# Loads in the order of use, indirect stores behind the stacks' loads, and experts' rows one tile ahead: a change to a two-layer transformer kernel

## The chip, the cores and the metric

One NeuronCore of a Trainium2 chip. The metric is the device time of one execution in microseconds (us), as the median of several runs. PE is the matrix engine (PEld its weight loads), DVE the vector engine, ACT the scalar engine, POOL the GpSimd engine, and SP the engine that issues most of the DMAs. Each engine works through its own list of instructions in order; an instruction that waits holds up all that stand behind it.

## The reference

Sixteen sequences of 512 rows of 256 go through two layers. Every step is `x = x + f(layernorm(x))` but the last, which has no norm.

```python
q, k, v = split(norm(x) @ Wqkv)               # layer 0: 16 heads of 16, rotary positions
w = softmax(q k^T / 4, keys at most 127 back)
x = x + (w v) @ Wout
s = norm(x) @ Wr.T + br                       # 8 experts, each row goes to its top 2
x = x + sum over the 2 of weight_e * ((silu(a_e) * b_e) @ Wl2[e] + bl2[e])
q = norm(x) @ Wq.T + bq                       # layer 1: causal over all 512 keys, biases
k = norm(x) @ Wv.T + bv ; v = norm(x) @ Wk.T + bk
x = x + softmax(q k^T / 16) v @ Wo.T + bo
x = x + x @ (round(weight / s) clipped to -1..1, times s)
```

## The kernel before

The program has three stages, one after the other: **a0** (attention with a window, the routing, and the storing of the normed rows in `xs`, sorted by expert), the **experts** (39 tiles of 512 rows of `xs`, results to `ys`), and **a1** (the gathering of each row's two results from `ys`, full attention, the ternary product). a0 and a1 are the same function `pipeline`.

`pipeline` first runs a block of preparation (L335 to L414): SP loads w, the tables, the identity, the masks, `wo` in 16 pieces, and the rest; ACT and DVE split w into a high and a low part (`wh`, `wl`), DVE sets the rows of ones in both `kst`, and in a1 forms the bias `boa` and the ternary weights. All engines meet at its end. Only then comes the block that does the work, and with it the load of x (L488).

The work on a sequence is some 25 kinds of steps, and a written table, `turn(i)`, gives each step a position between 0 and 1 in a turn. In turn i four sequences are in work: i+2 is normed, turned over, projected, rotated (`rope`), split into three bf16 parts (`part`, POOL L579 to L590) and stored (SP L496) to `parts_dram`, from where it comes back in another layout as `qst` and `kst` (`stack`, SP L506, 8 loads of 384 KB); i+1 has its scores formed for the row maxima (`S`, PE L1073, DVE L882), which go through `nmax_dram` into `qst` (`minus`: SP L511, a wait for the store, SP L513); i has its exponentials and products (`T`, PE L1095, ACT L675, PE L1113); i-1 is turned back (PE L1127, ACT L691), multiplied by `wo` (PE L1136), and in a0 normed again, scored and routed. The steps of a turn are sorted by position, and every engine walks this one `order`.

In a0 the last step of a turn is `scatter` (position 0.97): POOL L563 issues 8 indirect DMAs of 128 rows each. The loads of the stacks stand at 0.70 to 1.0. SP also carries the experts' weights through the core: a load (`fetch`, L470), a split on ACT and POOL, a store (`keep`, L475).

In a1 `gather(n, k)` is 4 indirect DMAs in a row on POOL (L570) into the 4 tiles of one buffer `yg`, and `mix(n, k, t)` is DVE's product of a tile with its gate, added to x (L729). The first `mix` waits for all 4 gathers, and the next `gather` for all 4 `mix`. x is loaded at 0.55 of a turn, the gathers stand at 0.35 and 0.81, the statistics at the start of the next turn.

The experts' loop is two steps unrolled. In each SP issues for tile m the rows (`xg`, L1239), w1 (L1245), w2 (L1248) and two biases (L1251, L1252). On PE come the transposes of `xg` (L1396), the first product (L1360) and the second one (L1374) of an earlier tile. There is one `xg`.

Of the kernel before, what the change touches and what calls it, by code (L numbers as in the profile page):

```python
# [105 lines left out]
def pipeline(nc, name, x_in, x_out, w_all, w_out, tables, biases, window, scale, consts, routed, mixed, ternary_w):  # L106
# [19 lines left out]
    nmax_d = nc.dram_tensor(f"{name}_nmax_dram", [2, 2, H, T], BF16, kind="Internal").ap()  # L126
# [21 lines left out]
    def turn(i):  # L148
# [11 lines left out]
        if 0 <= o < B:  # L160
# [3 lines left out]
            out += [(0.16 + 0.02 * t, ("stats2", o, t)) for t in range(NT)] + [(0.235, ("aggr2", o))]  # L164
            if routed:
                out += [(0.28 + 0.02 * t, ("norm2", o, t)) for t in range(NT)]
                out += [(0.15, ("y", o)), (0.50, ("turn2", o, 0)), (0.52, ("turn2", o, 1)), (0.58, ("score", o)),
                        (0.66, ("exp2", o)), (0.79, ("place", o)), (0.97, ("scatter", o))]
                out += [(0.615 + 0.0175 * k, ("gates", o, k)) for k in range(20)]
            else:  # L170
                out += [(0.27 + 0.015 * t, ("norm2", o, t)) for t in range(NT)]
                out += [(0.345, ("turn2", o, 0)), (0.36, ("turn2", o, 1)), (0.49, ("last", o, 0)), (0.51, ("last", o, 1)),
                        (0.515, ("final", o, 0)), (0.535, ("final", o, 1)), (0.54, ("y", o))]
# [11 lines left out]
        for n, at in ((m, -0.5),) * (m == 0) + ((m + 1, 0.55),) * (0 <= m + 1 < B):  # L185
            out.append((at, ("load", n)))
            if mixed:
                out += [(at - 0.2, ("gather", n, 0)), (at + 0.26, ("gather", n, 1))]
                out += [(at + 0.19 + 0.02 * t, ("mix", n, 0, t)) for t in range(NT)]
                out += [(at + 0.39 + 0.015 * t, ("mix", n, 1, t)) for t in range(NT)]  # L190
            else:
                out += [(at + 0.25 + 0.02 * t, ("stats", n, t)) for t in range(NT)] + [(at + 0.33, ("aggr", n))]
        if biases and 0 <= m < B:
            out.append((0.50, ("shift", m)))
        if 0 <= m < B:
            if mixed:
                out += [(0.005 + 0.02 * t, ("stats", m, t)) for t in range(NT)] + [(0.075, ("aggr", m))]
                out += [(0.125 + 0.015 * t, ("norm", m, t)) for t in range(NT)]
            else:
                out += [(0.03 + 0.02 * t, ("norm", m, t)) for t in range(NT)]  # L200
            out += [(0.20, ("turn", m, 0)), (0.215, ("turn", m, 1))]
            for a in range(2):
                p = 0.27 + 0.13 * a
# [6 lines left out]
    for i in range(-2, B + 1):  # L210
# [6 lines left out]
    with ctx:  # L217
# [34 lines left out]
        bvc = xn[:, 0, :].rearrange("p (c n) -> p c n", c=KC)  # L252
        bob = xn[:, 1, :]
        all_ones = xn[:, 2, 0:P]
# [21 lines left out]
        ot = sb("ot", [P, KC, T])  # L276
        if routed:
# [1245 lines left out]
```

## Time and profile before

| | us |
|---|---|
| median of 3 runs | 3257.35 (3247.95 to 3259.71) |
| the profiled execution | 3238.48 |
| its span | 3236.8 |
| busy PE, DVE, ACT, POOL | 2606.6, 1855.1, 1375.3, 922.1 |
| mean granted clock of PE | 0.90 |
| a0, from start to the last scatter's first DMA | 0 to 1101 |
| experts, first transposes to the start of a1 | 1130 to 1916 |
| a1 | 1916 to 3237 |

A row of the timeline has the start, the duration, engine, line and operation, out<-in, the count of instructions put together, and in brackets the idle time before it with what ended it; "issue" is a wait for nothing that the profile shows.

### The profile page before, as it was taken

How to read it: one execution, taken by the hardware profiler on the slowest of the kernel's cores; microseconds unless marked ns; L12 is line 12 of the kernel's file. 1: busy time of each engine (PE TensorE's matmuls, PEld its weight loads, DVE VectorE, ACT ScalarE, POOL GpSimd, SP SyncE). 2: the span in 40 equal slices, each digit the busy share in tenths (PEclk: the TensorE clock that was granted, in tenths of full speed). 3: DMA queues.
4: the chain of work that ended last, by engine and by line, in shares of the span. 5: the costliest groups of instructions: out<-in, count | busy, mean ns of one | idle time of the engine just before them, and what ended most of it. 6: DMA issues, size and time to landing. Idle time of an engine off the chain costs nothing. (4 is left out here: it accounts for less than half of the span.)

```text
span 3236.8 us, 51965 instructions
## 1 busy us (share of the span) xinstructions
PE 2606.6 (81%) x17726; PEld 1745.3 (54%) x17726; DVE 1855.1 (57%) x6538; ACT 1375.3 (42%) x2419; POOL 922.1 (28%) x862
## 2 busy tenths in 40 slices
PE   3788888888888399989899952788888888888887
PEld 2455555555555277778777851344444444444444
DVE  3767766775675344444444443666666666666661
ACT  1445544554554233333333311255555545555554
POOL 2434544544342200000000004343333333334300
PEclk8889988988899699999999975799999989999998
DMA  4565565565433565566666544334444433333330
GB/s 118 164 199 169 190 202 166 166 210 194 145 126 99 186 239 212 214 217 215 214 214 214 215 137 117 102 102 123 131 120 128 122 106 106 106 105 111 100 93 14
DMA packets 263344, 494.65 MB, mean 153 GB/s; under 512 B 27104, under 2 KB 194272, under 8 KB 253024
## 3 DMA queue, kind: packets, MB, share of 16 engines
q1 hardware_dynamic: 245232, 437.99, 42.3%
q0 software_dynamic: 17904, 54.02, 5.0%
q8 instruction: 114, 1.87, 0.2%
q14 instruction: 94, 0.77, 0.1%
HBM read 302.53 MB, written 189.40 MB: 152 GB/s over the span
## 5 line engine op out<-in xcount | busy, mean ns | idle before, releaser
L882 DVE CUSTOM_DVE_ANT_0 a_junk<-a_bank,a_smask 128x256 bf16<-128x256 f32 (+3 forms) x2048 | 812.8, 435 | 499.5 <-PE a_bank L1073 477.2
L675 ACT ACTIVATE a_pr<-a_bank 128x512 f32<-128x512 f32 (+1 forms) x1152 | 635.7, 574 | 698.6 <-PE a_bank L994 636.3
L1073 PE MATMUL a_bank<-a_kst,a_qst 96*128 96x256 bf16 (+3 forms) x2048 | 464.8, 302 | 203.1 <-DVE a_nmax L882 149.6
L1095 PE MATMUL a_bank<-a_qst,a_kst 98*128 98x256 bf16 (+3 forms) x2048 | 440.4, 292 | 24.9 <-ACT a_pr L675 21.5
L1073 PEld LDWEIGHTS a_bank<-a_kst,a_qst 96*128 96x128 bf16 x2048 | 172.3, 102 | 457.9 <-DVE a_nmax L882 263.0
L1360 PE MATMUL e_bank<-e_xh,e_w 128*128 128x512 f32 x1248 | 402.9, 405 | 1.4 <-DVE e_xl L1341 1.4
L1113 PE MATMUL a_bank<-a_pr,a_va 128*32 128x256 f32 (+3 forms) x4096 | 365.9, 435 | 40.9 <-ACT a_pr L675 36.5
L994 PE MATMUL a_bank<-a_mask,a_identb 128*128 128x512 bf16 (+2 forms) x1152 | 356.1, 309 | 0.0
L1333 DVE SCALAR_TENSOR_TENSOR e_gf<-e_bank,e_b,e_sa 128x512 f32<-128x512 f32 x156 | 117.2, 751 | 280.5 <-ACT e_sa L1304 280.5
L1095 PEld LDWEIGHTS a_bank<-a_qst,a_kst 98*128 98x128 bf16 x2048 | 183.1, 101 | 152.5 <-ACT a_pr L675 72.0
L1304 ACT ACTIVATE e_sa<-e_bank,e_b 128x512 f32<-128x512 f32 x156 | 107.4, 689 | 371.5 <-PE e_bank L1360 371.3
L1360 PEld LDWEIGHTS e_bank<-e_xh,e_w 128*128 128x128 f32 x1248 | 237.3, 195 | 50.5 <-DVE e_xl L1341 1.8
L1360 PE MATMUL e_bank<-e_xl,e_w 128*128 128x512 f32 x624 | 250.3, 401 | 0.0
L1282 POOL DMA_DIRECT2D ys<-e_yt x39 | 29.5, 757 | 771.2 <-DVE e_yt L1322 752.1
L1374 PE MATMUL e_bank<-e_w,e_gh 128*128 128x256 f32 x1248 | 222.8, 279 | 2.9 <-DVE e_gl L1337 2.9
L1374 PEld LDWEIGHTS e_bank<-e_w,e_gh 128*128 128x128 f32 x1248 | 193.0, 189 | 4.9 <-DVE e_gl L1337 3.4
L1113 PEld LDWEIGHTS a_bank<-a_pr,a_va 128*32 128x32 f32 x4096 | 84.8, 111 | 186.9 <-issue 92.6
L570 POOL DMA_INDIRECT a_yg<-ys,a_yrow x128 | 124.2, 970 | 196.8 <-DVE a_xt L729 137.5
L1374 PE MATMUL e_bank<-e_w,e_gl 128*128 128x256 f32 x624 | 173.8, 279 | 0.0
L1337 DVE TENSOR_TENSOR e_gl<-e_gf,e_gh 128x512 fp32r<-128x512 f32 x156 | 108.1, 693 | 109.9 <-ACT e_gh L1309 109.9
L882 DVE DVE_READ_ACCUMULATOR2_ANT a_nmax<- 128x1 f32 x2048 | 169.7, 83 | 0.0
L1136 PE MATMUL a_bank<-a_wo,a_ot 128*128 128x256 f32 x512 | 155.2, 457 | 15.5 <-ACT a_ot L691 14.7
(168 smaller groups left out, 4494.7 us busy)
## 6 DMA issues: line engine op xcount, KB each, us to landing
e_w<-ws_dram SPq DMA_DIRECT2D x39, 2048.0 KB, 9.5
a_parts_dram<-a_parts SPq DMA_DIRECT2D x224, 256.0 KB, 4.0
a_qst<-a_parts_dram SPq DMA_DIRECT2D x128, 384.0 KB, 9.9
a_kst<-a_parts_dram SPq DMA_DIRECT2D x128, 384.0 KB, 11.1
e_w<-ws_dram SPq DMA_DIRECT2D x39, 1024.0 KB, 6.0
a_parts_dram<-a_parts SPq DMA_DIRECT2D x32, 768.0 KB, 3.8
ws_dram<-a_ws SPq DMA_DIRECT2D x24, 1024.0 KB
e_xg<-xs SPq DMA_DIRECT2D x39, 512.0 KB, 6.0
```

Source lines behind the costliest of these rows:

```text
L570: pool.indirect_dma_start(yg[:, t, :], None, ys, bass.IndirectOffsetOnAxis(ap=yrow[:, k, m * NT + t:m * NT + t + 1], axis=0))\
L675: nc.scalar.activation(pr[b][:, h:h + per, :], TB_[at % 2][:, 0:per * w].rearrange("p (h w) -> p h w", h=per), ACT.Exp, scale=scale).then_ ...
L882: last = nc.vector.tensor_tensor_reduce(junk[:, at % 2, j * w:(j + 1) * w], SB_[at % 2][:, j * w:(j + 1) * w], smask[:, T - w:T], scale=-1 ...
L994: return nc.tensor.matmul(out, identb[:, :], rhs, start=False, stop=True, skip_group_check=True)
L1073: last = nc.tensor.matmul(out[:, j * w:(j + 1) * w], q[0:ROWS, hh, qb * P:(qb + 1) * P], k[0:ROWS, hh, k0:k0 + w], start=True, stop=True)
L1095: nc.tensor.matmul(out[:, j * w:(j + 1) * w], k[0:AUG, hh, b * P:(b + 1) * P], q[0:AUG, hh, q0:q0 + w], start=(j == 0), stop=False, skip_g ...
L1113: last = nc.tensor.matmul(PVB[32 * j:32 * (j + 1), q0:q0 + w], va[i % 2][:, b, (g * HG + j) * VW:(g * HG + j) * VW + 32], pr[b][:, j, :], ...
L1136: last = nc.tensor.matmul(WB[n][:, (t % 2) * D:(t % 2 + 1) * D], ot[:, c, t * P:(t + 1) * P], wo[:, c, :], start=(c == 0), stop=(c == KC - 1))
L1333: nc.vector.scalar_tensor_tensor(gf[f % 2][:, :], BB[f % 2][:, :], b1[s.slot][:, FC + f:FC + f + 1], sa[f % 2][:, :], ALU.add, ALU.mult).t ...
L1337: nc.vector.tensor_tensor(gl[s.slot][:, f, :], gf[f % 2][:, :], gh[s.slot][:, f, :].bitcast(F32), ALU.subtract).then_inc(gl_done, 1)
L1360: last = nc.tensor.matmul(out[:, :], first(s.slot, low)[:, kc, col:col + P], x[s.slot][:, kc, :], start=(p == 0), stop=(p == 3 * KC - 1))
L1374: last = nc.tensor.matmul(YB[n][:, (t % 2) * D:(t % 2 + 1) * D], x[s.slot][:, f, t * P:(t + 1) * P], second(s.slot, low)[:, f, :], start=( ...
```

## The change

Five things, in all three stages.

1. **No block of preparation.** x, w and the identity are loaded first, then the rest; `wo` in 4 pieces; in a1 yrow and gate before all. The rows of ones come by two DMAs from a tile that DVE fills. Each engine waits for what it needs: DVE's first `rope` waits for all constants. `boa` and the ternary weights become steps of the order (`bias` at 0.22 of the turn of sequence 0's projection, `quantise` at the start of the next).
2. **The maxima** go from `nmt` into `qst` in one DMA, without `nmax_dram` and without SP's wait.
3. **Scatters** stand at 0.115 to 0.213 of the next turn, and each waits until the stacks of sequence r+3 have landed.
4. **a1's table:** gathers and mixes tile by tile, with a semaphore for each tile; load of x at 0.435; statistics at the end of the turn; norm, turn, project and the last steps of the turn earlier, the second half's projection later.
5. **Experts:** SP issues w1 of tile m, then the rows of tile m+1, then w2 of m.

```diff
+                out += [(0.155 + 0.015 * t, ("stats2", o, t)) for t in range(NT)] + [(0.21, ("aggr2", o))]
...
-                        (0.66, ("exp2", o)), (0.79, ("place", o)), (0.97, ("scatter", o))]
+                        (0.66, ("exp2", o)), (0.79, ("place", o))]
...
+                out += [(0.235 + 0.015 * t, ("norm2", o, t)) for t in range(NT)]
+                out += [(0.31, ("turn2", o, 0)), (0.325, ("turn2", o, 1)), (0.37, ("last", o, 0)), (0.385, ("last", o, 1)),
+                        (0.40, ("final", o, 0)), (0.415, ("final", o, 1)), (0.42, ("y", o))]
+        if routed and 0 <= i - 2 < B:
+            out += [(0.115 + 0.014 * k, ("scatter", i - 2, k)) for k in range(2 * NT)]
...
-        for n, at in ((m, -0.5),) * (m == 0) + ((m + 1, 0.55),) * (0 <= m + 1 < B):
+        for n, at in ((m, -0.5),) * (m == 0) + ((m + 1, 0.55 if routed else 0.435),) * (0 <= m + 1 < B):
             out.append((at, ("load", n)))
             if mixed:
-                out += [(at - 0.2, ("gather", n, 0)), (at + 0.26, ("gather", n, 1))]
-                out += [(at + 0.19 + 0.02 * t, ("mix", n, 0, t)) for t in range(NT)]
-                out += [(at + 0.39 + 0.015 * t, ("mix", n, 1, t)) for t in range(NT)]
+                for t in range(NT):
+                    out += [(at - 0.165 + 0.025 * t, ("gather", n, 0, t)), (at + 0.125 + 0.02 * t, ("mix", n, 0, t)),
+                            (at + 0.135 + 0.025 * t, ("gather", n, 1, t)), (at + 0.285 + 0.02 * t, ("mix", n, 1, t)),
+                            (at + 0.365 + 0.02 * t, ("stats", n, t))]
+                out.append((at + 0.465, ("aggr", n)))
...
+            if mixed:
+                sp.dma_start(yrow[:, :, :], yrow_d).then_inc(index_loaded, 16)
+                sp.dma_start(gate[:, :, :], gate_d).then_inc(index_loaded, 16)
+            sp.dma_start(xt[0][:, :, :], x_in[0].rearrange("(t p) d -> p t d", p=P)).then_inc(x_loaded[0], 16)
+            sp.dma_start(w_raw, w_all).then_inc(w_loaded, 16)
+            sp.dma_start(ident[:, :], ident_d).then_inc(ident_loaded, 16)
+            for dst, src in loads:
+                sp.dma_start(dst, src).then_inc(const_loaded, 16)
+            sp.wait_ge(ones_done, 1)
+            for i in range(2):
+                sp.dma_start(kst[i][ROWS:AUG, :, :], junk[0:2 * H, 0, :]).then_inc(ones_loaded, 16)
...
-                    sp.dma_start(nmax_d[s % 2, half], nmt[half][:, :]).then_inc(nmax_stored, 16)
-                    sp.wait_ge(nmax_stored, 16 * (2 * s + half + 1))
-                    sp.dma_start(qst[s % 2][ROWS:AUG, half * H // 2:(half + 1) * H // 2, :],
-                                 nmax_d[s % 2, half].rearrange("(r h) n -> r h n", r=2))\
+                    sp.dma_start(qst[s % 2][ROWS:AUG, half * H // 2:(half + 1) * H // 2, :], nmt[half][:, :])\
                         .then_inc(nmax_loaded[s % 2][half], 16)
...
+                    if r + 3 < B:
+                        pool.wait_ge(stack_loaded[(r + 3) % 2][NG - 1], 32 * ((r + 3) // 2 + 1))
+                    pool.indirect_dma_start(
+                        xs, bass.IndirectOffsetOnAxis(ap=row[r % 2][:, k, t:t + 1], axis=0),
+                        rn[r % 2][:, t, :], None).then_inc(scattered[r % 2], 16)
...
+                    pool.wait_ge(mixed_in, max(0, NT * (2 * m + k - 1) + t + 1))
...
+                    if (m, a, half) == (0, 0, 0):
+                        dve.wait_ge(const_loaded, 16 * len(loads))
+                        dve.wait_ge(ones_loaded, 32)
+                        dve.wait_ge(fills, 6)
...
-                def weights_of(m, e):
+                def weights_of(m, e, between):
                     sp.wait_ge(ab_done, (m + -1).count(FC))
                     sp.sem_inc(carrier, 1)
                     sp.dma_start(w[m.slot][:, :, 0:N1], ws_d[e][:, :, 0:N1]).then_inc(w1_loaded[m.slot], 16)
+                    if between:
+                        between()
                     sp.wait_ge(y_projected, (m + -1).count(2))
...
+                        weights_of(m, e, None if final else lambda: rows_of(after, r))
```

Where the scatters stand: POOL's list in a steady turn of a0, of the kernel before.

```order
L539 TENSOR_SCALAR a_lean<-a_mv 128x4
L540 TENSOR_SCALAR a_ve<-a_mv 128x4
L542 TENSOR_TENSOR a_rstd<-a_ve,a_power 128x4
L544 TENSOR_TENSOR a_shift<-a_lean,a_rstd 128x4
L563 DMA xs<-e_rn,e_row 69632x256 x8
L550 TENSOR_SCALAR a_lean<-a_mv 128x4
L551 TENSOR_SCALAR a_ve<-a_mv 128x4
```

The same place after the change, with the semaphores that an instruction waits for.

```order
L481 TENSOR_SCALAR a_lean<-a_mv 128x4 [waits a0_xn_done,a0_var_done]
L482 TENSOR_SCALAR a_ve<-a_mv 128x4
L484 TENSOR_TENSOR a_rstd<-a_ve,a_power 128x4 [waits a0_ve_done]
L486 TENSOR_TENSOR a_shift<-a_lean,a_rstd 128x4 [waits a0_rstd_done]
L505 DMA xs<-e_rn,e_row 69632x256 [waits a0_stack_loaded13,a0_rows_done] x8
L492 TENSOR_SCALAR a_lean<-a_mv 128x4 [waits a0_xn2_done,a0_var2_done]
L493 TENSOR_SCALAR a_ve<-a_mv 128x4
```

POOL's own order is the same; the wait for `stack_loaded` is what moves the scatters.

The experts' step on SP, before (ISA rows are waits and increments).

```order
L1239 DMA e_xg<-xs 128x4x256
L1243 ISA
L1245 ISA
L1245 DMA e_w<-ws_dram 128x2x2048
L1246 ISA
L1248 ISA
L1248 DMA e_w<-ws_dram 128x2x1024
L1249 ISA
L1251 ISA
L1251 DMA e_b<-in_be 128x8
```

And after; the `e_xg` is that of the next tile.

```order
L1256 DMA e_w<-ws_dram 128x2x2048
L1248 ISA
L1250 ISA
L1250 DMA e_xg<-xs 128x4x256
L1259 ISA
L1261 ISA
L1261 DMA e_w<-ws_dram 128x2x1024
L1262 ISA
L1264 ISA
L1264 DMA e_b<-in_be 128x8
```

The rows of a tile have moved from ahead of its own w1 to between the w1 and the w2 of the tile before.

Gathers in a1 on POOL, before.

```order
L570 DMA a_yg<-ys,a_yrow 128x256 x4
L586 TENSOR_TENSOR a_qk<-a_qk,a_parts 128x1024
L579 TENSOR_TENSOR a_qk<-a_rt 128x512
L580 TENSOR_TENSOR a_qk<-a_rt 128x512
L590 TENSOR_TENSOR a_parts<-a_qk,a_parts 128x1024
L595 TENSOR_TENSOR a_xt<-a_xt,a_boa 128x1024
```

And after.

```order
L540 TENSOR_TENSOR a_xt<-a_xt,a_boa 128x1024
L513 DMA a_yg<-ys,a_yrow 128x256
L529 TENSOR_TENSOR a_qk<-a_qk,a_parts 128x1024
L513 DMA a_yg<-ys,a_yrow 128x256 x2
L533 TENSOR_TENSOR a_parts<-a_qk,a_parts 128x1024
L513 DMA a_yg<-ys,a_yrow 128x256
```

The four gathers of one k no longer stand together; they are spread between the steps that split the parts.

## Rows read from the trace of the kernel before

**Rows 1.** The profile's page: busy time of each engine.

```profile
PE 2606.6 (81%) x17726; PEld 1745.3 (54%) x17726; DVE 1855.1 (57%) x6538; ACT 1375.3 (42%) x2419; POOL 922.1 (28%) x862
```

**Rows 2.** Timeline, start of a0.

```profile
0.85 0.41 SPq L340 DMA_DIRECT2D a_rt<-in_w  x1
...
5.35 1.47 ACT L361 CAST a_wh<-a_rt 128x1536 fp32r<-128x1536 f32 x1 [3.22 <-DMA a_rt<-in_w]
...
18.32 1.76 DVE L373 TENSOR_TENSOR a_wl<-a_rt,a_wh 128x1536 fp32r<-128x1536 f32 x1
...
20.57 0.38 SPq L488 DMA_DIRECT2D a_xt<-in_x  x1
24.50 1.41 DVE L713 BATCH_NORM_STATS2 a_stats<-a_xt 128x6 f32<-128x256 f32 x4 [4.43 <-DMA a_xt<-in_x]
...
33.97 0.76 PE L989 MATMUL a_bank<-a_xh,a_wh 128*128 128x512 f32 x1 [1.49 <-DVE a_xl L857]
```

**Rows 3.** Timeline, end of one turn of a0 and start of the next.

```profile
470.41 0.55 SPq L506 DMA_DIRECT2D a_qst<-a_parts_dram  x1
...
475.20 1.09 POOL L563 DMA_INDIRECT xs<-e_rn,e_row  x1 [0.67 <-DVE e_row L849]
...
483.76 0.59 ACT L691 COPY a_ot<-a_bank 128x512 f32<-128x512 f32 x1 [1.78 <-remote]
...
484.40 1.12 PE L1127 MATMUL a_bank<-a_ident,a_on 128*128 128x128 f32 x4 [3.96 <-issue]
...
500.95 0.24 POOL L550 TENSOR_SCALAR a_lean<-a_mv 128x4 f32<-128x4 f32 x1 [15.79 <-DVE a_mv L741]
```

**Rows 4.** Windows: stretch, length, busy times, granted clock, DMA share, GB/s.

```profile
484.00:492.00 8.00, 6.12 (x18) 4.23 (x19) 0.78 (x4) 1.93 (x4) 0.96 (x1) 0.50 0.64 219
...
475.00:487.00 12.00, 6.98 (x56) 5.37 (x54) 2.76 (x17) 5.08 (x11) 7.83 (x8) 0.83 1.03 316
```

**Rows 5.** Idle time before PE L1127 (PE and PEld together), 220 to 1000 us.

```profile
  issue: 85.2, 25
```

**Rows 6.** DMA queues, 470 to 492 us: packets, MB, share of 16 engines.

```profile
q8 instruction: 1, 0.02, 0.3%
```

**Rows 7.** Waits of SP, 180 to 1040 us: total, times, longest.

```profile
SPq L513 <- DMA a_nmax_dram<-a_nmt: 52.1, 28, 3.7
```

**Rows 8.** Experts: timeline, idle before L1396 in 1160 to 1900 us, and windows.

```profile
1405.92 0.39 SPq L1239 DMA_DIRECT2D e_xg<-xs  x1
...
1412.04 1.09 PE L1396 MATMUL e_bank<-e_ident,e_xg 128*128 128x128 f32 x8 [1.79 <-DMA e_xg<-xs]
...
  DMA e_xg<-xs: 66.8, 36
...
1412.04:1431.40 19.36, 17.56 (x104) 15.22 (x104) 8.31 (x12) 6.31 (x10) 0.75 (x1) 1.00 0.61 214
1431.40:1452.00 20.60, 19.20 (x104) 16.64 (x104) 7.76 (x12) 6.31 (x10) 0.75 (x1) 0.92 0.58 199
1169.31:1868.71 699.40, 634.01 (x3640) 548.79 (x3641) 291.13 (x421) 219.63 (x350) 26.44 (x35) 0.97 0.61 217
```

**Rows 9.** Timeline, start of a1.

```profile
1916.23 0.34 SPq L340 DMA_DIRECT2D a_rt<-in_w  x1
...
1943.21 1.04 POOL L570 DMA_INDIRECT a_yg<-ys,a_yrow  x1 [24.14 <-POOLq L337]
...
1958.43 1.67 DVE L729 SCALAR_TENSOR_TENSOR a_xt<-a_yg,a_gate,a_xt 128x256 f32<-128x256 f32 x4 [6.83 <-issue]
...
1969.50 0.77 PE L989 MATMUL a_bank<-a_xh,a_wh 128*128 128x512 f32 x1 [1.49 <-DVE a_xl L857]
```

**Rows 10.** A turn of a1: windows, PE's waits (2090 to 3050), idle before DVE L729 (2000 to 3100).

```profile
2469.00:2543.31 74.31, 62.78 (x430) 35.61 (x429) 48.82 (x178) 38.06 (x71) 26.97 (x26) 0.91 0.39 115
...
PE a_bank L1073 <- DVE a_nmax L882: 75.5, 74, 4.2
...
  issue: 111.1, 15
```

More of the change, by code:

```diff
@@ L163, in turn @@
                     (0.145, ("add", o, 1))]
-            out += [(0.16 + 0.02 * t, ("stats2", o, t)) for t in range(NT)] + [(0.235, ("aggr2", o))]
+            if routed:
+                out += [(0.16 + 0.02 * t, ("stats2", o, t)) for t in range(NT)] + [(0.235, ("aggr2", o))]
+            else:
+                out += [(0.155 + 0.015 * t, ("stats2", o, t)) for t in range(NT)] + [(0.21, ("aggr2", o))]
             if routed:
@@ L194, in turn @@
             out.append((0.50, ("shift", m)))
+        if biases and m == 0:
+            out.append((0.22, ("bias",)))
+        if mixed and s == 0:
+            out.append((0.0, ("quantise",)))
         if 0 <= m < B:
[L196 to L201, printed above, removed]
+            out += [(0.03 + 0.02 * t, ("norm", m, t)) for t in range(NT)]
+            out += [(0.18 if mixed else 0.20, ("turn", m, 0)), (0.195 if mixed else 0.215, ("turn", m, 1))]
             for a in range(2):
-                p = 0.27 + 0.13 * a
+                p = 0.24 + 0.19 * a if mixed else 0.27 + 0.13 * a
                 out += [(p, ("project", m, a)), (p + 0.04, ("rope", m, a, 0)), (p + 0.065, ("rope", m, a, 1)),
@@ L209, in pipeline @@
     order = []
-    for i in range(-2, B + 1):
+    for i in range(-2, B + 2):
         order += merged([turn(i)])
@@ L435, in pipeline @@
         plan_step = sem("plan_step")
-        gathered = sem("gathered")
+        gathered = [sem(f"gathered{t}") for t in range(NT)]
         mixed_in = sem("mixed_in")
@@ L704, in choices @@
                 return v.unsqueeze(1).broadcast_to([P, 2, NT, NE])
-            for st in order:
-                if st[0] == "stats":
+            nc.vector.memset(junk[:, 0, :], 1.0).then_inc(ones_done, 1)
+            if routed:
+                nc.vector.memset(ones[:, :], 1.0)
+                for e in range(NE):
+                    nc.vector.memset(numbers[:, e:e + 1], float(e))
+                nc.vector.memset(taken[:, :], 0.0).then_inc(set_done, 1)
+                dve.wait_ge(set_done, 1)
@@ L994, in mask_it @@
                 return nc.tensor.matmul(out, identb[:, :], rhs, start=False, stop=True, skip_group_check=True)
+            pe.wait_ge(ident_loaded, 16)
             for st in order:
-                if st[0] == "turn":
+                if st[0] == "bias":
+                    pe.wait_ge(const_loaded, 16 * len(loads))
+                    pe.wait_ge(bias_step, 1)
+                    for c in range(KC):
+                        last = nc.tensor.matmul(TRB[:, 0:D], bvc[:, c, :], wo[:, c, :], start=(c == 0), stop=(c == KC - 1))
+                    last.then_inc(bias_step, 1)
+                elif st[0] == "quantise":
+                    pe.wait_ge(tern_step, 1)
+                    nc.tensor.matmul(TRB[:, 0:1], all_ones, rowsum, start=True, stop=True).then_inc(tern_step, 1)
+                elif st[0] == "turn":
                     m, c = st[1:]
@@ L1156, in turns_of_two @@
     step(Seq(None, 1), Seq(None, 2))
-    with fori(1, (count - 1) // 2) as pair:
+    with fori(1, (count - 1) // 2 - 1) as pair:
         for c in range(2):
             step(Seq(pair, c), Seq(pair, c + 1))
+    for c in range(count - 3, count - 1):
+        step(Seq(None, c), Seq(None, c + 1))
     step(Seq(None, count - 1), None)
```

220 lines of the change are left out of this document (98 added, 122 removed).

## The prediction

> **What bounds the kernel now.** I read the page first. PE is busy for 2606.6 of 3236.8 us, and no other engine for more than 1855.1 [rows 1]. So the 630 us in which PE stands are what an edit of waits can take back, together with the time that PE works at less than full clock: the mean granted clock is 0.90. The next views were the windows and the timelines at the places that the diff touches. They show five sorts of loss, one for each part of the change.
>
> **Start of a0.** The block of preparation puts everything in a row. w is issued at 0.85 and ACT's cast starts at 5.35, but DVE forms `wl` only at 18.32, behind its memsets, and x is asked for at 20.57, after the block's end. The statistics start at 24.50 and the first product of the projection at 33.97 [rows 2]. After the change x and w are issued together at the start. w then shares the DMA engines with x; I take the cast 1.5 us later, at 6.9. Cast 1.5 and `wl` 1.8 end at 10.1, and `wl` stands ahead of the statistics on DVE. From statistics to product it takes 33.97 - 24.50 = 9.5 us, so the product comes at about 19.5: **14.5 us saved**. The other constants (13 fewer DMAs with 4 pieces of `wo` for 16, and ones by DMA) are wanted by the first `rope`, 3 us behind the product. A start is one occurrence; at worst they land some us late, at best w is not slowed, so 8 to 18.
>
> **Turns of a0.** A turn takes some 63 us. The stacks' loads are issued from 470.41 on, and the scatter's eight DMAs start at 475.20 [rows 3], on top of them. From 475 to 487 the DMA share is 1.03 [rows 4]. In its second half PE stands for 3.96 us ahead of L1127 for "issue", and ACT at L691 for "remote" [rows 3]: not for a semaphore's data, and on two engines at once. The queue view of that stretch has an instruction queue with one packet of 0.02 MB [rows 6]. My reading is that the engines' next instructions come by the same DMA engines and are late when those are full. After the stall PE works at a granted clock of 0.50 from 484 to 492, with 6.12 us busy [rows 4]; at full clock that work is 3.1. The stall comes in all 13 turns that have both a scatter and stacks behind it: L1127 waits 85.2 us for issue there, PE and PEld counted together, so some 3.5 to 4 us a turn [rows 5]. The second turn, which has stacks and no scatter, doesn't have it.
>
> After the change the scatters wait for the last stack. The eight stacks are 8 x 384 KB, at 316 GB/s [rows 4] about 10 us, so they land near 481 to 483, and the eight scatters end 10 us later, near 492. POOL has nothing else to do until 500.95 [rows 3], so its own queue is not held up. The gain is at most 4 + 3 = 7 us a turn, or 7.5 with SP's waits; the stacks alone still fill the DMA engines for 10 us, so a bit of the stall may stay. I take 6: 13 x 6 = **78 us**. Bounds: 0, if the stacks alone do it, and 98. The copy of the maxima without `nmax_dram` takes SP's wait away, 52.1 us over 28 times, 1.9 each [rows 7]. SP has gaps behind it and the maxima are needed only in the next turn, so I cost it at nothing; the keep and the stacks start up to 2 us earlier, and would be what it costs or gives.
>
> On this the Trainium skill speaks against the change: "DMA: Bandwidth & Descriptors", section "Queues, rings and completion order", says that each DMA engine goes round its queues packet by packet. By that rule an instruction packet waits for a packet of each queue and not for the scatter's end, and moving the scatter would give nearly nothing; the sum would be 78 us smaller. The pattern of turns with and without a scatter speaks the other way, so I keep the gain, with that as a rival.
>
> **Experts.** From 1169.31 to 1868.71 there are 35 tiles in 699.40 us, 19.98 each [rows 8]. The rows of a tile are issued at 1405.92, and PE waits for them with its transposes until 1412.04; over the stage that is 66.8 us in 36 waits. The tile that starts at 1412.04 has full clock, and 17.56 busy in 19.36; the next has a clock of 0.92, and 19.20 in 20.60 [rows 8]. With the rows one tile ahead, they are issued once the one `xg` has been read, some 2 us into a tile, and have 15 us to land. PE then has no wait left and works at full clock: 17.56 a tile. 35 x (19.98 - 17.56) = **84 us**. SP's w2 now stands behind that issue, but it isn't due before the second product of the tile before has ended, which is later. The DMA share goes from 0.61 to 0.61 x 19.98 / 17.56 = 0.69. Bounds: 67, the waits alone, and 88.
>
> **Start of a1.** The first DMA is at 1916.23, the first gather at 1943.21, the last mix at 1958.43, the first product at 1969.50 [rows 9]: 53.3 us. After the change yrow is loaded first, so the gathers start some 3 us in, and the eight gathers and mixes, tile by tile, take at most the 16.9 us from 1943.21 to the mixes' end at 1960.1. Tile by tile the second gathers overlap the first mixes, so I take 15.4. The 9.4 us to the product follow: 3 + 15.4 + 9.4 = 27.8, and **25.5 us saved**. Bounds 18 to 30. The bias and the ternary steps, about 8 us of DVE, move under PE's work.
>
> **Turns of a1.** A turn takes 74.31 us with 62.78 of PE busy at a clock of 0.91 [rows 10], so the work is 57 us at full clock. PE's largest wait is for DVE's maxima, 75.5 us over 13 turns, 5.8 a turn. DVE stands for the gathers at L729 for 111.1 us over 15 turns, 7.4 each [rows 10], since all four must land before the first mix and it waits in order with the maxima behind it. Gathers spread over the turn take that away. The half of it reaches PE, since scores have a buffer: 3.7, and 1.3 for the dips of the clock around it, 5 a turn, 14 turns: **70 us**. Bounds: 0, if another wait of DVE takes its place, and 8 a turn, 112.
>
> **The sum.** 14.5 + 78 + 84 + 25.5 + 70 = 272. The profiled execution took 3238.5; 3238.5 - 272 = 2966.5. It lies 18.9 us under the median of the runs, so the forecast of the median is **2985 us**. The ends of a0 and a1 and the passage to the experts are untouched: nothing there.
>
> **The rivals.**
> A, *the stall at the turn's start stays*: the stacks alone fill the DMA engines, or the instructions are late for another reason. For it: the stacks are 3 MB and the scatter 1 MB. Against it: the turn without a scatter. 2985 + 78 = 3063.
> B, *a1's turns gain nothing*: DVE has 48.82 us of work a turn and ACT 38.06 [rows 10], tied to PE both ways; a mix spread over the order can stand ahead of the maxima eight times in place of two. 2985 + 70 = 3055. A and B together: 3133.
> C, *all of it comes back*, clocks included: 20 us more in a0 and 42 in a1, 2923.
> D, *slower*: POOL, in order, waits for the stacks with the second norm's steps (L550) behind it. Its slack is 500.95 - 492 = 9 us. If the stacks landed 25 us later than I think, 16 us a turn would be lost, 13 x 16 = 208, and the 78 not won; from 15 us a turn on this eats the other 194. At 20 us a turn: 3238.5 - 194 + 260 + 18.9 = 3323. The loads would have to run at a third of the rate in the rows, so it is unlikely.
> E, *it doesn't do what it says*: POOL's order of scatters is the same as before, and only the semaphore moves them; had the stacks landed before `rows_done`, nothing would move. But the last is issued at 475.13 and the first scatter at 475.20, so it binds. For a0 that is A's time.
>
> **How the numbers follow.** Forecast 0.50, A (with E) 0.17, B 0.12, both 0.06, C 0.11, D 0.02, and 0.02 for all small gains lost at once. The range runs from just under C, 2905, to between the single rivals and both together, 3105; it leaves out A with B, D and the tails. A measurement can tell some 0.5% (16 us) from no change. Even A with B is 124 us faster, as the experts and the two starts rest on waits that are plainly seen. Faster 0.96, same 0.02, slower 0.02.
>
> **What would show it.** In the changed profile: the first product at about 19.5 us; no wait of 4 us ahead of PE's turn-back in a0, a DMA share that falls after the stacks and rises again, and turns of 57 us; expert tiles of 17.6 us with clock 1.00 and no wait for `xg`; a1's first product 28 us after its first DMA; a1's turns at 69 us, with DVE's idle time before the mix near 0. I am wrong if a0's turns stay at 63 us, if a1's stay at 74, or if POOL's wait at the scatter reaches the second norm.

## The result and the profile after

| | before | after |
|---|---|---|
| median of the runs, us | 3258.53 (4 runs) | 3124.55 (3122.26 to 3126.09, 4 runs) |
| profiled execution, its span | 3238.48, 3236.8 | 3123.75, 3122.1 |
| a0, to the first DMA of the experts | 1116.2 | 1115.6 |
| experts | 800.0 | 705.0 |
| a1 | 1320.6 | 1301.5 |

The ratio is 0.959 (0.956 to 0.962): faster by 134 us at the median and by 115 us from profile to profile (the profiled execution of before was quicker than each of its four runs). The forecast was 2985 us, 273 us less; the measured time is outside its range of 2905 to 3105, and within 9 us of the rivals A and B together, 3133. Of the runs further down, that of `best_spread` which was profiled stood at a granted clock of 0.64 throughout (3651 us for 2964), so its turns are not given, and such executions are left out of every ratio.

The profile's page of the changed kernel, busy times, against [rows 1]:

```profile
PE 2560.2 (82%) x17553; PEld 1726.6 (55%) x17726; DVE 1865.9 (60%) x6536; ACT 1375.2 (44%) x2419; POOL 927.0 (30%) x863
```

PE lost 46 us of busy time, 28 of them in the experts, where it now works at full clock; the rest can't be told from the 173 matrix products that the trace of after lacks. DVE, of which nothing was asked that wasn't before, was busy for 11 us more, and in a1 alone for 23. That turns out to be a clue.

**Starts.** Timeline, start of a0, against [rows 2]:

```profile
0.84 0.44 SPq L393 DMA_DIRECT2D a_xt<-in_x  x1
...
7.04 1.47 ACT L547 CAST a_wh<-a_rt 128x1536 fp32r<-128x1536 f32 x1 [4.91 <-DMA a_rt<-in_w]
...
8.62 1.76 DVE L664 TENSOR_TENSOR a_wl<-a_rt,a_wh 128x1536 fp32r<-128x1536 f32 x1 [6.85 <-ACT a_wh L547]
...
19.90 0.77 PE L981 MATMUL a_bank<-a_xh,a_wh 128*128 128x512 f32 x1 [1.49 <-DVE a_xl L845]
```

The cast comes at 7.04 (forecast 6.9), the first product at 19.90 (19.5). In a1 the first DMA is at 1820.58 and the first product at 1853.83: 33.3 us for 53.3 before (forecast 27.8).

```profile
1820.58 0.33 SPq L391 DMA_DIRECT2D a_yrow<-yrow_dram  x1
...
1848.65 1.94 PE L1004 MATMUL a_bank<-a_ident,a_xn 128*128 128x128 f32 x8 [33.90 <-ACT a_xn L561]
1852.34 2.05 PE L994 MATMUL a_bank<-a_wo,a_ot 128*128 128x256 f32 x4 [1.76 <-DVE a_ot L670]
1853.83 0.99 PE L981 MATMUL a_bank<-a_xh,a_wh 128*128 128x512 f32 x1
```

The bias's product (L994) now stands in PE's list between the turning over and the projection. The 3.2 us from the end of the turning over (1850.6) to the product hold it; a wait of 1.49 us stands in that place in a0, so some 1.7 us are its own.

**Experts.** A window of 34 tiles, and the idle time before the transposes, against [rows 8]:

```profile
1157.58:1747.00 589.42, 589.42 (x3537) 520.12 (x3536) 281.09 (x408) 211.27 (x340) 25.76 (x34) 1.00 0.72 250
```

```profile
  DMA e_xg<-xs: 33.3, 1
```

A tile takes 17.34 us each time, PE is busy for the whole of it at full clock, and the one wait that is left is that for the first tile.

**Turns of a0.** They did not get shorter. From the rows of sequence 0 to those of sequence 12 are 12 turns: 63.2 us each before, 64.7 after. The timeline of a turn of the changed kernel, against [rows 3]:

```profile
472.86 1.09 POOL L505 DMA_INDIRECT xs<-e_rn,e_row  x1 [12.26 <-DMA a_kst<-a_parts_dram]
...
481.86 0.96 POOL L505 DMA_INDIRECT xs<-e_rn,e_row  x1 [0.31 <-issue]
...
482.89 0.27 PE L1122 MATMUL a_bank<-a_pr,a_va 128*32 128x128 f32 x1 [1.04 <-issue]
...
482.92 0.59 ACT L590 CAST a_xh<-a_bank 128x512 fp32r<-128x512 f32 x1 [1.54 <-remote]
...
486.29 0.76 PE L981 MATMUL a_bank<-a_xh,a_wh 128*128 128x512 f32 x1 [3.13 <-DVE a_xl L845]
```

And the windows, against [rows 4]:

```profile
480.00:485.00 5.00, 1.48 (x17) 0.63 (x13) 1.29 (x4) 1.82 (x4) 2.21 (x3) 0.89 0.23 82
485.00:490.00 5.00, 3.71 (x9) 2.97 (x10) 2.25 (x12) 2.92 (x5) 2.79 (x5) 0.50 0.02 5
```

The scatters wait for the stacks and start in nearly idle DMA engines (a share of 0.19 from 472 to 476). The stall went from PE's turn-back, as forecast, and came back in front of the projection: again at the end of the eight scatters, again with a clock of 0.50 behind it, but now at a DMA share of 0.23. Full DMA engines were not its cause.

Nor were late instructions, as the prediction read out of [rows 6]. These are the DMA queues of the changed kernel from 473 to 486 us, and no instruction queue is among them, though ACT and PE came back to work within that time:

```profile
q0 software_dynamic: 384, 1.05, 23.0%
q1 hardware_dynamic: 528, 0.52, 11.5%
```

I call it a halt where PE, DVE and ACT all stand for over 0.8 us. In the 12 turns the changed kernel has 10 of them, and in none did an instruction packet land, nor in the 1 us ahead; the kernel before has 17, and 14 of those are without one. None begins before the fifth of the eight scatters.

**Turns of a1.** 75.1 us each, where before had 74.2 (mean of 12). The window of one turn, against [rows 10]:

```profile
2402.34:2477.45 75.11, 62.38 (x429) 34.70 (x429) 51.40 (x178) 38.35 (x70) 27.14 (x25) 0.91 0.39 113
```

DVE is busy for 51.4 us instead of 48.8. The timelines of DVE, POOL and PE in the middle of that turn show where the 2.6 us went:

```profile
2438.98 1.16 DVE L884 CAST a_nparts<-a_nmax 128x32 bf16<-128x32 f32 x1
2440.18 2.28 DVE L886 TENSOR_TENSOR a_nparts<-a_nmax,a_nparts 128x32 bf16<-128x32 f32 x1
...
2444.56 2.67 DVE L717 SCALAR_TENSOR_TENSOR a_xt<-a_yg,a_gate,a_xt 128x256 f32<-128x256 f32 x1
```

```profile
2440.07 2.35 POOL L540 TENSOR_TENSOR a_xt<-a_xt,a_boa 128x1024 f32<-128x1024 f32 x1
...
2444.80 2.13 POOL L529 TENSOR_TENSOR a_qk<-a_qk,a_parts 128x1024 f32<-128x1024 f32 x1
```

```profile
2443.20 0.50 PE L1082 MATMUL a_bank<-a_kst,a_qst 96*128 96x384 bf16 x1 [2.75 <-DVE a_nmax L874]
2447.76 0.50 PE L1082 MATMUL a_bank<-a_kst,a_qst 96*128 96x384 bf16 x1 [2.13 <-DVE a_nmax L874]
```

L886 takes 0.19 us elsewhere and L717 0.47. Here both end within 0.3 us of POOL's step beside them (2442.46 and 2442.42; 2447.23 and 2446.93), and behind each PE stands. L884, which has one input, takes 1.16 for 0.18.

Of the three only the held mix (L717) is new. In the kernel before, L886's counterpart is as slow, and no mix is; its timeline, and its mixes from 2000 to 3100 us (shortest, median and longest in ns):

```profile
2409.98 2.06 DVE L894 TENSOR_TENSOR a_nparts<-a_nmax,a_nparts 128x32 bf16<-128x32 f32 x1
...
L729 DVE SCALAR_TENSOR_TENSOR a_xt<-a_yg,a_gate,a_xt x117: 474/481/486, 1999.9 to 3032.0; 128x256 f32<-128x256 f32 x117
```

Over 12 turns, what DVE's instructions took beyond their shortest is 5.3 us a turn after and 2.5 before; 2.2 of the 2.8 between them are one held mix a turn. DVE's wait for gathers, 7.4 us a turn in [rows 10], is gone as forecast, but what it gave was spent again.

### The profile page after: what moved, and what is told of

Its sections match the earlier page's. It is cut to its first block and busy times, and to the rows that moved or that the text cites. A ratio compares the mean times of both kernels' runs of the same rounds, so it can differ in the third digit from the quotient of the medians.

```text
span 3122.1 us, 51758 instructions
## 1 busy us (share of the span) xinstructions
PE 2560.2 (82%) x17553; PEld 1726.6 (55%) x17726; DVE 1865.9 (60%) x6536; ACT 1375.2 (44%) x2419; POOL 927.0 (30%) x863
## 5 line engine op out<-in xcount | busy, mean ns | idle before, releaser
L625 ACT ACTIVATE a_pr<-a_bank 128x512 f32<-128x512 f32 (+1 forms) x1152 | 643.7, 575 | 771.3 <-PE a_bank L986 573.1
L1379 PE MATMUL e_bank<-e_xh,e_w 128*128 128x512 f32 x1248 | 390.7, 394 | 1.4 <-DVE e_xl L1360 1.4
L986 PE MATMUL a_bank<-a_mask,a_identb 128*128 128x128 bf16 (+2 forms) x979 | 288.4, 295 | 0.0
L1379 PEld LDWEIGHTS e_bank<-e_xh,e_w 128*128 128x128 f32 x1248 | 229.4, 189 | 48.7 <-DVE e_xl L1360 1.8
L505 POOL DMA_INDIRECT xs<-e_rn,e_row x128 | 126.4, 988 | 266.0 <-DMA a_kst<-a_parts_dram 162.4
L533 POOL TENSOR_TENSOR a_parts<-a_qk,a_parts 128x1024 bf16<-128x1024 f32 x64 | 139.2, 2175 | 93.3 <-ACT a_parts L600 93.0
```

The costliest lines, as they stand in the source:

```text
L505: pool.indirect_dma_start(xs, bass.IndirectOffsetOnAxis(ap=row[r % 2][:, k, t:t + 1], axis=0), rn[r % 2][:, t, :], None).then_inc(scattere ...
L533: nc.gpsimd.tensor_tensor(parts[:, a, 2], qk[:, a], parts[:, a, 1], ALU.subtract)\
L625: nc.scalar.activation(pr[b][:, h:h + per, :], TB_[at % 2][:, 0:per * w].rearrange("p (h w) -> p h w", h=per), ACT.Exp, scale=scale).then_ ...
L986: return nc.tensor.matmul(out, identb[:, :], rhs, start=False, stop=True, skip_group_check=True)
L1379: last = nc.tensor.matmul(out[:, :], first(s.slot, low)[:, kc, col:col + P], x[s.slot][:, kc, :], start=(p == 0), stop=(p == 3 * KC - 1))
```

## The experiments

The runs were made on four chips, I to IV, so a kernel is compared by its ratio to the kernel before on the same chip, and stages by their profiles. "Turn" is the mean of 12 turns, in the same place of each profile (before: 63.2 and 74.2; after: 64.7 and 75.1). Apart from that first pair, the two kernels of the change were profiled on chip III alone; a difference to them from another chip can be the chip's: the kernel before has turns of 74.2 in a1 in the first profile and of 75.1 on III.

| kernel | chip | median, before there | ratio (95%) | turn of a0 | turn of a1 |
|---|---|---|---|---|---|
| s_nowait | I | 3109, 3248 | 0.957 (0.954 to 0.960) | 63.9 | 75.1 |
| s_direct | I | 3036, 3248 | 0.935 (0.933 to 0.937) | 58.4 | 75.1 |
| a1_old | I | 3060, 3248 | 0.943 (0.940 to 0.946) | 64.2 | 69.8 |
| nmax_dram | I | 3120, 3248 | 0.961 (0.958 to 0.963) | 63.9 | 75.1 |
| best_spread | II | 2964, 3176 | 0.934 (0.931 to 0.936) | | |
| g_direct | II | 2957, 3176 | 0.932 (0.929 to 0.934) | 57.9 | 68.2 |
| a1_half | II | 2991, 3176 | 0.942 (0.940 to 0.944) | 58.4 | 70.4 |
| a1_shift | II | 3024, 3176 | 0.952 (0.950 to 0.954) | 58.1 | 73.8 |
| before_b | III | 3257, 3260 | 0.999 (0.997 to 1.000) | 64.1 | 75.1 |
| after_b | III | 3124, 3260 | 0.957 (0.954 to 0.959) | 64.7 | 75.1 |
| x_old | III | 3221, 3260 | 0.986 (0.984 to 0.989) | 64.3 | 75.1 |
| best2 | III | 2984, 3260 | 0.914 (0.911 to 0.916) | 58.3 | 69.4 |
| s_one | IV | 3044, 3250 | 0.935 (0.933 to 0.937) | 58.3 | 75.1 |
| s_two | IV | 3098, 3250 | 0.952 (0.950 to 0.954) | 62.5 | 75.1 |
| s_four | IV | 3082, 3250 | 0.947 (0.946 to 0.949) | 61.4 | 75.1 |

**s_nowait: the wait for the stacks taken out**

```diff
-                    if r + 3 < B:
-                        pool.wait_ge(stack_loaded[(r + 3) % 2][NG - 1], 32 * ((r + 3) // 2 + 1))
```

> The changed kernel without the scatters' wait for the stacks' loads: they are issued as soon as the rows are known, on top of the stacks, as in the kernel before. Theory 1 (the stacks' loads and the scatter together fill the DMA engines and hold up the instructions): a0's turns, 65.3 us in the changed kernel, go up or stay, and the 4 us ahead of PE's turn-back come back. Theory 2 (each scatter costs its turn about 4 us wherever it stands, and the wait adds some 2 us by laying it on the second norm and the projection): a0's turns go to about 63.3 us, 13 x 2 = 26 us less, about 3098 us.

0.957 for the change's 0.959, and turns of 63.9 us. `nmax_dram` and `a1_old`, which keep the wait and ran on the same chip, have 63.9 and 64.2, so the wait does nothing that can be told. The waits of some 4 us (2.7 to 5.4) ahead of PE's turn-back came back and those ahead of the projection went: the wait moves the halt and no more. That is what theory 1 said would be seen, and it doesn't tell what halts the engines; with the scatters on top of the stacks the turn is no longer than with both apart, which speaks against full DMA engines.

**s_direct: plain stores in place of indirect ones**

```diff
-                    pool.indirect_dma_start(
-                        xs, bass.IndirectOffsetOnAxis(ap=row[r % 2][:, k, t:t + 1], axis=0),
-                        rn[r % 2][:, t, :], None).then_inc(scattered[r % 2], 16)
+                    at = (k * NT + t) * REGION + r * P
+                    pool.dma_start(xs[at:at + P, :], rn[r % 2][:, t, :]).then_inc(scattered[r % 2], 16)
```

> The changed kernel with each indirect store of 128 rows replaced by a plain store of the same 128 rows from the same queue to a fixed place (so the rows are not sorted by expert; eight stores of 1 MB at the first sequence give the unwritten rows a value, and the pads wait for all but the last rows). Theory 1 (bytes on full DMA engines): no change, turns of 65 us. Theory 2 (the indirect form, which POOL works out row by row, is what halts ACT and PE for 1.5 to 4 us near the end of the eight): the halts go and a0's turns fall by 2 to 6 us, 26 to 78 us in all.

As many bytes from the same queue at the same place in the turn (to fixed rows, so what the experts get is wrong, and a0's work is the same). The turn is 5.5 to 5.8 us shorter than in `nmax_dram` and `a1_old` on the same chip, and 6.3 shorter than the changed kernel's in the first profile; PE's clock in one turn is 0.97, and 0.90 in the changed kernel's from 460.80 to 526.60. POOL's row in the timeline of s_direct:

```profile
454.40 4.36 POOL L510 DMA_DIRECT2D xs<-e_rn  x8 [11.05 <-DMA a_kst<-a_parts_dram]
```

And the window of one turn, and that of the stacks' loads ahead of the stores:

```profile
443.55:500.31 56.76, 51.08 (x428) 32.74 (x428) 44.22 (x199) 32.29 (x58) 26.25 (x26) 0.97 0.67 205
...
444.00:454.00 10.00, 7.92 (x63) 6.31 (x62) 3.03 (x20) 5.57 (x11) 0.00 (x0) 1.00 1.02 257
```

Eight plain stores are issued in 4.4 us, eight indirect ones in 10. None of the halts is left; the one place where PE, DVE and ACT stand for over 0.8 us (at 249 us, in the turn to which this kernel adds 8 MB of stores) is a wait for loaded data. In the second window the DMA engines are full for 10 us, and PE's longest wait there is 1.5 us, for ACT. It is the indirect form that halts the engines, not the bytes.

**a1_old: a1's steps at their old positions**, the diff being that of the change, turned round, for the branches of a1.

> The changed kernel with the positions of a1's steps as in the kernel before (gathers and mixes keep their semaphore for each tile). Theory 1 (the new table crowds DVE with mixes, rotations and statistics between 0.45 and 0.65 of a turn, and PE waits there): turns of a1 go from 75.1 to 74 us or less, 14 us or more off. Theory 2 (another limit binds in a1, the table matters nothing): 75 us as in the changed kernel. If per-tile waits alone were worth my 5 us, the turns would be 69 us and the whole 85 us less.

The turn falls from 75.1 (also in the other kernels of this chip with the new table) to 69.8, by 5.3 us. That is 4.4 below the kernel before in the first profile and 5.3 below it on III. So the semaphores for each tile, with gathers that still stand in rows of four, bring what the prediction counted on (5 a turn), and the new table takes it away again.

**nmax_dram: the maxima through DRAM again**

```diff
+                    sp.dma_start(nmax_d[s % 2, half], nmt[half][:, :]).then_inc(nmax_stored, 16)
+                    sp.wait_ge(nmax_stored, 16 * (2 * s + half + 1))
```

> The changed kernel with the row maxima again sent through DRAM (a store, a wait of SP, a load). Theory 1 (as in the prediction, worth nothing): within 5 us of the changed kernel. Theory 2 (the earlier start of the keep and the stacks moves DMA load to a worse place): some 10 to 25 us faster. Theory 3 (SP's 1.9 us waits did hold up stacks): 10 to 25 us slower.

0.961 against 0.959 for the change on another chip, intervals over each other: worth nothing that can be told, as costed.

**best_spread: a1_old, scatters without the wait and one at a time**

```diff
-            out += [(0.115 + 0.014 * k, ("scatter", i - 2, k)) for k in range(2 * NT)]
+            out += [(0.115 + 0.08 * k, ("scatter", i - 2, k)) for k in range(2 * NT)]
```

> a1_old, and in a0 the scatters without the wait for the stacks and one at a time, every 0.08 of a turn from 0.115 to 0.675 (some 5 us apart). Theory 1 (the halt comes from eight indirect stores in a row, as a backlog): the halts of 1.5 to 4 us go, a0's turns fall from 65 towards the 58 us of the plain stores, so some 60 to 90 us less than a1_old's 3060. Theory 2 (each indirect store costs its 0.9 us, wherever it is): turns stay at 63 to 65 us, about 3045 to 3060.

0.934 against 0.943 for a1_old, but on another chip, and that one has to be understood first: there the kernel before takes 3176 us, and its neighbours a1_half and a1_shift, with the scatters exactly as the change has them, show turns of 58 us.

**g_direct: a1_old with plain loads in place of gathers**

```diff
-                    pool.indirect_dma_start(
-                        yg[:, t, :], None, ys,
-                        bass.IndirectOffsetOnAxis(ap=yrow[:, k, m * NT + t:m * NT + t + 1], axis=0))\
-                        .then_inc(gathered[t], 16)
+                    at = ((m * NT + t) * 2 + k) * P
+                    pool.dma_start(yg[:, t, :], ys[at:at + P, :]).then_inc(gathered[t], 16)
```

> a1_old with each indirect gather of 128 rows replaced by a plain load of as many rows from a fixed place, from the same queue (so wrong rows are mixed in). Theory 1 (only indirect stores halt the other engines; no halts are seen at the gathers): a1's turns stay at 70 us, at most 1 us less, 0 to 14 us in all. Theory 2 (the indirect form costs 7 us a turn in a1 too): turns of 63 us, 90 us less.

68.2 us a turn, 1.6 less than a1_old, which ran on another chip (I). Nothing like the 7 us of theory 2, a little more than theory 1 said. As chip II shows no halts at the stores either, what gathers in a row cost on the other chips stays open; that such a row can halt the engines there is seen below, in before_b.

**a1_half: old positions for load, gathers, mixes, statistics and first norm alone**

```diff
-        for n, at in ((m, -0.5),) * (m == 0) + ((m + 1, 0.55 if routed else 0.435),) * (0 <= m + 1 < B):
+        for n, at in ((m, -0.5),) * (m == 0) + ((m + 1, 0.55),) * (0 <= m + 1 < B):
```

> The changed kernel with the old positions only for a1's load, gathers, mixes, statistics and first norm; projection, second norm and last steps stay where the change put them. Theory 1 (the mixes at 0.56 to 0.78, on top of POOL's long steps and DVE's rotations, are what costs): turns fall from 75 to about 70 us, 60 us less. Theory 2 (the later second projection at 0.43 and the earlier last steps are what costs): turns stay at 74 to 75 us.

70.4 us: nearly all of the 5.3, though on another chip. The projection and the last steps can stay where the change put them; it is the mixes and what goes with them. No mix takes over 0.49 us here, while the counterpart of L886 still takes up to 2.28.

**a1_shift: POOL's bias elsewhere**

```diff
-            out.append((0.50, ("shift", m)))
+            out.append((0.62, ("shift", m)))
```

> The changed kernel with POOL's addition of the bias (2.35 us, between SBUF tensors) at 0.62 of a turn in place of 0.50. In the changed kernel DVE's two small steps on the maxima take 1.16 and 2.28 us where they meet POOL's long steps, and one of a turn's mixes 2.67, against 0.18, 0.19 and 0.47 else. Theory 1 (DVE is held by POOL's step until that ends): the 2.28 us go to 0.19 or show up at another DVE step that the bias now meets; turns fall by up to 2 us, 0 to 28 us in all. Theory 2 (they are slow for another reason): they stay slow wherever the bias is.

Turns of 73.8, 1.3 less than with the change's table on the other chips. L886 in 2000 to 2900 us, and L717:

```profile
L886 DVE TENSOR_TENSOR a_nparts<-a_nmax,a_nparts x25: 191/193/194, 2012.7 to 2893.8; 128x32 bf16<-128x32 f32 x25
```

```profile
L717 DVE SCALAR_TENSOR_TENSOR a_xt<-a_yg,a_gate,a_xt x88: 472/482/2660, 2056.0 to 2808.7; 128x256 f32<-128x256 f32 x88
```

With nothing changed on DVE, L886 is at 0.19 us in all 25 cases, while in the changed kernel about one of two took 2.28. Some mixes still take 2.66: they meet POOL's steps now. DVE is held by POOL's step until that has ended. This is what the Trainium skill says in "SBUF — State Buffer", section "Who interferes with whom": a DVE instruction with two SBUF inputs contends with a GpSimd instruction that reads SBUF, since they share a port pair that one of them locks for its whole instruction; the rows agree, L886 and L717 having two such inputs. Which of the two has to go first these rows don't tell: L717's own starts 0.24 us before POOL's L529, at the end of a gather that POOL issued.

**before_b and after_b: both kernels on one more chip**

> The kernel before, profiled again on the chip of this call. Two chips were seen so far: on one the kernel before takes 3248 to 3258 us, and ACT and PE halt at the indirect stores; on the other it takes 3176 us, and the changed kernel's a0 has turns of 58 us with no such halt. Theory 1 (the halts at indirect stores belong to the chip, not to the kernel): where the time is near 3176, no halt of 4 us ahead of PE's turn-back and turns of a0 near 58 us; where it is near 3250, halts and 63 us. Theory 2 (the halts belong to the kernel before on every chip): 63 us and the halts here too.

> The changed kernel, profiled again on the chip of this call. Theory 1 (the halts belong to the chip and both kernels have them): ratio to before 0.96 on either chip, turns of a0 equal in both kernels to within 2 us. Theory 2 (the change takes the halts away where they are): the ratio is lower than 0.959 on one of the chips.

Chip III is one of 3260 us, and there the kernel before has turns of 64.1 and the changed one 64.7; the ratio is 0.957. So both have the halts on a chip that has them, 16 and 11 in 12 turns. On chip II the a0 of a1_half and a1_shift, which is the changed kernel's, has none, and the kernel before is 84 us faster than on III, about 13 turns of 6; it was not profiled there, so it is not shown that the halts make up the 84. Chips I and III had the halts with eight in a row, and so had the profiled pair of above, whose chip isn't known. On IV no kernel with eight in a row was profiled; its time for the kernel before, 3250, is that of the others.

In a1 a row of four gathers halts the engines too. In before_b PE, DVE and ACT all stand for 0.65 us in each of 12 turns, always 5.1 us after the start of the first gather of a row (here at 2216.45):

```profile
2221.55:2222.20 0.65, 0.01 (x1) 0.00 (x0) 0.00 (x0) 0.00 (x0) 0.00 (x0) 1.00 1.01 221
```

It is the row of each turn that has stacks' loads beside it, at a share near 1; the other, at 0.28 (2187.96 to 2193), has no such place, and neither has the changed kernel, where the gathers stand apart.

**x_old: the experts' rows as before**

```diff
-                        weights_of(m, e, None if final else lambda: rows_of(after, r))
+                        rows_of(m, row_of(m))
+                        weights_of(m, e, None)
```

> The changed kernel with the experts' rows issued as before, at the start of their own tile's loads. If the rows one tile ahead are worth what the profiles say (800.0 us for the stage before, 705.0 after), the stage goes back to about 800 us and the kernel is 95 us slower than the changed one. The rival: part of the gain came from something else (the stage's start or the peeled loop), and it is only 60 to 80 us slower.

3221 for 3124: 97 us. The stage goes from 705.3 to 809.4 us, and even 10 over that of the kernel before on this chip (799.5), which wasn't looked into. The stage's whole gain is that of the rows' place in SP's list.

**best2: best_spread with the bias at 0.64**

> best_spread (old table of a1, scatters spread and without the wait) with POOL's bias at 0.64 of a turn of a1. In a1_old DVE's step on the maxima still takes 2.06 us beside POOL's split, and PE waits 2.18 us behind it once a turn. Theory 1 (the port, once free there, gives this back): a1's turns fall from 70 to 68 us, about 28 us less, ratio 0.925. Theory 2 (the steps only meet elsewhere): 70 us, ratio 0.934 as best_spread.

A ratio of 0.914 (0.911 to 0.916), 276 us below the kernel before and 140 below the change, on a chip with halts. a0's turns are 58.3. a1's are 69.4, 0.4 less than a1_old's on chip I: L886 is at 0.19 always, but the turn hardly gains, and L884 now takes up to 1.70, so theory 2 for a1. That the gain beyond best_spread's ratio is that of the spreading, which can't show on chip II, is likely and not shown apart.

**s_one, s_two, s_four: rows of one, two and four**, without the wait for the stacks, each row starting 0.08 of a turn later for each scatter ahead of it. That of s_two:

```diff
-            out += [(0.115 + 0.014 * k, ("scatter", i - 2, k)) for k in range(2 * NT)]
+            out += [(0.115 + 0.08 * 2 * (k // 2) + 0.0001 * (k % 2), ("scatter", i - 2, k)) for k in range(2 * NT)]
```

> The changed kernel, only the scatters without the wait and one at a time, 0.08 of a turn apart (a1 as the change has it). Theory 1 (a row of indirect stores halts the others, single ones don't): turns of a0 of 58 to 59 us where the changed kernel has 65, 80 us less. Theory 2 (best2's short turns of a0 came from something else): 63 us or more. If the chip is one on which no halts are seen, all three kernels of this call have 58.

> As s_one, but in four pairs, 0.16 apart. Theory 1a (each further store of a row costs about 1 us, 7 us for eight): turns of a0 of about 61 to 62 us. Theory 1b (the halt comes only once some four or more stand in a row): turns of 58 to 59 us.

> As s_one, but in two rows of four, 0.32 apart. Theory 1a (each further store of a row costs): about 64 us. Theory 1b (the halt comes only past some length): between 58 and 65 us, and the trace shows at which store of the row ACT and PE first halt.

On chip IV. One at a time (the first two still follow each other): 58.3 us a turn, as with plain stores. A window of such a turn:

```profile
493.56:552.31 58.75, 51.74 (x437) 33.08 (x430) 45.64 (x198) 32.71 (x58) 29.86 (x26) 0.97 0.63 198
```

Spreading alone does it; it is the row that halts the others. Pairs gave 62.5 and fours 61.4, eights 64.7 on other chips. That is not a price for each further store: pairs and fours have no halt over 0.8 us in 12 turns, and fours have two of 0.4, 5.3 us after the row's start. Their turns are longer by another way. In s_two POOL's pair stands just ahead of four long steps without a gap, and DVE's small cast on the maxima lasts until the last of them has ended:

```profile
493.70 6.95 DVE L882 CAST a_nparts<-a_nmax 128x32 bf16<-128x32 f32 x1
...
498.49 2.11 POOL L527 TENSOR_TENSOR a_qk<-a_qk,a_parts 128x1024 f32<-128x1024 f32 x1
...
501.62 0.61 PE L1080 MATMUL a_bank<-a_kst,a_qst 96*128 96x256 bf16 x2 [3.08 <-DVE a_nmax L872]
```

PE stands 3.08 us behind it, and goes on at a lower clock (0.89 in this turn, 0.97 in that of s_one, where a scatter stands between those steps and the cast takes 3.69). In s_four the row of four makes POOL late, ACT waits 4.08 us for it and PE 1.98 for ACT, and a DVE step of 0.19 us (L746) takes 3.70. So halts begin some 5 us after the start of a row, as far as these runs show, and theory 1b was nearer; what the shorter rows cost here lies in where they put POOL's other steps. No run takes the two apart, and that chip IV would halt at eight is read from its time for the kernel before alone.

## Why the prediction was wrong

**Start of a0, 14.5 us: right** (14.1), by its steps: cast at 7.04 for 6.9, product at 19.90 for 19.5.

**Turns of a0, 78 us: the step that failed.** "After the change the scatters wait for the last stack. ... The gain is at most 4 + 3 = 7 us a turn." The turn became 1.5 us longer. The size of the stall was right: without it a turn is 5.5 to 6.4 us shorter than with eight in a row on the same chip (s_direct on I, best2 on III). The cause was not. I took the full DMA engines for it because they were full at that time, and the one packet of an instruction queue for evidence; the halts of the changed kernel end without one. The scatters were there too, and I only asked what the stacks would do without them. The turn without a scatter that I leaned on fits both readings. With the cause unmoved, a later place only moves the stall. Rival A had the time of this term right, but neither of its reasons was it: not the stacks alone (s_direct), and not late instructions. The rule of the Trainium skill that was weighed there ("DMA: Bandwidth & Descriptors", "Queues, rings and completion order") would have given the right number for this term; whether by its own mechanism, no run here shows.

**Experts, 84 us: right, mis-sized by 11.** A tile takes 17.34, not 17.56, which makes 92 us of the 35 tiles (why the window that I took had 0.2 us more, I can't show), and the rest of the stage gave 3: 95 us in the profile, 97 by x_old. The bound above, 88, was too low.

**Start of a1, 25.5 us: 20.0.** The eight gathers and mixes and the norm took 28 us to the first transpose, and the bias's product came ahead of the projection (1.7 us).

**Turns of a1, 70 us: the second that failed.** "Gathers spread over the turn take that away" was right, and worth what I said: a1_old gains 4.4 us a turn over the kernel before of the first profile, and 5.3 over that on III. But I priced the semaphores and not the table. The new positions put the mixes on top of POOL's long steps. One mix a turn is now held for 2 us, besides the split of the maxima, which was held before too, and PE stands behind both, 2.75 and 2.13 us in the turn shown. So -5 became +1 in the first pair, and 0 on III. With the old positions for the mixes and what goes with them it comes back (a1_half); how much of that is the held mix and how much the crowding, no run tells apart. Rival B had this as "another wait of DVE", without the port; that L894 took 2.06 us at 2409.98 in the kernel before, beside POOL's L586, could have been read.

**The maxima, nothing: right** (nmax_dram). **Rivals D and E**: POOL did wait for the stacks, until 472.86, and was through at 482.8; the second norm's steps came at 486.98, on DVE's account.

**The sum** of the terms as the profiles show them: 0.6 in a0 (14.1 of the start and 7.6 more up to the rows of sequence 0, less 18.0 in twelve turns and 3.1 in the rest), 95.1 in the experts, 19.1 in a1 (36.5 up to the first output's store, whose place in the turn is earlier too, less 17.4 from there to the last one's): 115 us. Two of the terms were independent and each had 0.17 or 0.12 against it; both fell, for which the range had no room.

## What to carry to other kernels

A stall that falls together with a full resource is not yet caused by it: look for a turn in which the other candidate is there alone, and if there is none, replace that one by its plain form before building a change on it. Spread indirect DMAs from POOL between its other steps, and don't issue them in a row. When a table of positions is made over, look at DVE's short instructions (with two SBUF inputs, and here a cast with one) and POOL's long ones side by side: where they overlapped here, the short one lasted until the long one had ended, through four of them where they stood without a gap, and what waits behind DVE pays. And issue a tile's rows one tile ahead where its one buffer is free early: that was most of what this change gained.

## What the hardware showed that I had not expected

Eight indirect stores of 128 rows of 1 KB in a row cost 6 us of a turn by halting ACT, DVE and PE near their end, at a DMA share of 0.23 as at 1.03, on chips I and III and in the first pair. On chip II the same row has none of it, and the kernel before is 2.5% faster there (3176 for 3257 us). A row of four gathers beside the stacks' loads halted them too, for 0.65 us a turn. The plain stores are issued in 0.55 us each, the indirect ones in 1.26. What in the halts differs from chip to chip, and through what the DMAs reach ACT, DVE and PE, was not tried; in the changed kernel it was no instruction packet.
